# Sums moved to node order by a 0/1 matrix on TensorE, in an eight-layer graph network

## The chip, the cores and the metric

One core of one Trainium2 chip runs one program. The metric is the device time of a whole execution in microseconds. The kernel before took 10204.36 us, the median of 3 runs (10197.07 to 10204.97).

## What is computed

A graph of N = 6250 nodes with 128 features and 100000 edges, sorted by their destination dst. Eight layers of message passing stand one behind the other, in four blocks; each block normalises (layer norm and relu) and ends in a residual. Every layer gathers the source row of each edge and reduces per destination.

```python
h = relu(layernorm(x));  x = x + relu(h @ Wself.T + mean(h[src] by dst) @ Wneigh.T + b)        # k=0
h = relu(layernorm(x));  m = h[src] * edge_feat * bf(edge_weight) * cut
x = x + ssp(segment_prod(m, dst) @ W3 + b3)                                                  # k=1
h = relu(layernorm(x));  three times: h = mean(h[src] by dst) @ Wl + h @ Wr + b  (relu twice) # k=2,3,4
x = x + h
h = relu(layernorm(x));  three times:                                                        # k=5,6,7
    t = h @ W;  alpha = leaky(al_s[src] + al_d[dst] + al_e), with a self loop per node
    coef = softmax of alpha over the edges of each dst;  h = bn(leaky(sum(t[src] * coef) + b))
x = x + h
```

## The kernel before, in words

**Tiles.** The edges are 784 tiles of 128 (ET, padded), taken in 98 groups of eight (NG, HT). The nodes are 49 tiles of 128 rows (NT), and node work goes in seven chunks of seven tiles (NCH, CH; a chunk is CW = 896 columns). X, T, G and H are node-sized buffers of 49 x 128 columns, acc is as large and is addressed by rank (below). The edge layers are k = 0, 2, 3, 4 (mean, `SAGE`), k = 1 (product) and k = 5, 6, 7 (attention, `GAT`).

**A pass of a layer.** POOL issues one indirect DMA per tile (L620, in attention L641), which gathers 128 rows from the layer's table in DRAM into one of two halves of `rows`; a half is a group. DVE makes a 0/1 matrix `onehot` of a group's positions (L1240; in attention L1287, times the weight), PE multiplies rows by it into a half of PSUM (L903, in attention L923), and DVE adds the eight 128-column windows into acc at offsets that it loads into registers (L1256, L1307). POOL gathers into a half again when its products are through. The offset is a rank: the number of distinct destinations before, so that sorted edges fill the columns of acc without holes. In the product pass (k = 1) messages are built and scanned instead of summed, and stored as rows.

**Nodes and ranks.** Nodes without edges have no rank, so acc must be spread to node order. In pass 0 ACT stages three numbers per edge (L792, meta_buf: dst and position where it is a segment's last, and 1), PE multiplies them by the same onehot (L905), and DVE adds them in the same way into macc, a part of H. At the pass's end PE transposes them (L1072), DVE works out `cmap` (the rank of each node), first and last position and count, and POOL scatters and SP reloads a table of them (L657).

**Between two passes** (a turn, in the prediction's word). ACT copies acc chunk by chunk (L732), PE multiplies it by the layer's weights (L888), DVE copies the product out (L1380), SP stores it to seg_rows, and POOL gathers 49 tiles of rows by cmap (L677) into G. DVE then works through G by chunks (mean_layer; attention_layer, with batch statistics over all nodes and sums on PE) and writes H, the next layer's input, which SP stores as the next table. After layer 0, normalize and its root on ACT are in the chunk too; after layer 1 they work on the whole of X at once. In attention the last messages' maxima come first: 49 gathers of at_last (L664) stand behind the pass on POOL.

**A layer's own product** (h @ W). ACT copies a chunk of H (L708), PE transposes it (L862), ACT copies that (L699), PE multiplies (L868, L871), DVE copies it to T (L1218, L1231). In k = 0 and 2 this stands before the pass, in k = 3 to 7 inside the turn, chunk by chunk behind mean_layer and attention_layer; in attention T is also the table that is gathered.

**Staging in attention.** The messages' weights need all of alpha first, so the first SG = 30 groups are gathered, sent from `rows` to DRAM by DMAs that ACT issues (L811), and taken back during the weighted pass. POOL's third group waits for the first of them.

The order of the work is written out by hand, engine by engine, with semaphores; the lines of the profile are those of the block below. The two places that set the attention layers' start on ACT and POOL are:

```python
                    elif g < SG + 2:
                        pool.wait_ge(*staged_by(l, g - 2))
...
                elif k in by_chunks:
                    stage_chunks(k)
```

Of the kernel before, what the change touches and what calls it, by code (L numbers as in the profile page):

```python
# [21 lines left out]
ALU = mybir.AluOpType  # L22
# [36 lines left out]
SG = 30  # L59
FG = NG - SG  # L60
GROUP_WORDS = HT * D
SCATTER_AFTER = 8
SAGE = (0, 2, 3, 4)
# [3 lines left out]
def build(nc, a, out):  # L67
    ds = bass.ds
    with ExitStack() as ctx:
# [14 lines left out]
        seg_rows = dram("seg_rows", (NPAD, D))  # L84
        flats = dram("flats", (4, EPAD))
# [4 lines left out]
        node_table = dram("node_table", (NPAD, 4))  # L90
# [14 lines left out]
        meta_buf = sb("meta_buf", [P, BT * 3])  # L105
# [22 lines left out]
        node_info = sb("node_info", [P, NT * 4])  # L128
        cmap = sb("cmap", [P, NT], I32)
# [11 lines left out]
        ids_int = sb("ids_int", [P, NT], I32)  # L141
# [10 lines left out]
        H3 = H[:, 0:NT * D].rearrange("p (t f) -> p t f", f=D)  # L152
        stage = onehot[:].rearrange("p a b -> p (a b)")
        stage_in, stage_mid = stage[:, 0:CW], stage[:, 1024:1024 + CW]
        stage_out = rows[:].rearrange("p a b -> p (a b)")[:, 0:CW]
        macc = H[0:3, :]
        meta_t = G[:, 0:3 * ET]
# [25 lines left out]
        for l in range(3):  # L183
# [9 lines left out]
                      4: mat(M["agg2"]), 5: ident[:], 6: ident[:], 7: ident[:]}  # L193
# [41 lines left out]
        blocks = acc[0:TB, 0:4 * NB * P].rearrange("p (q b c) -> p q b c", q=4, c=P)  # L235
        pos_i = acc[:, 5600:5600 + ET].bitcast(I32)
        dst_t, last_t, srcf_t = scan_tmp(T, 0), scan_tmp(T, 1), scan_tmp(T, 2)
# [23 lines left out]
        info3 = node_info[:].rearrange("p (t c) -> p t c", c=4)  # L261
# [25 lines left out]
        info_turned = sem("info_turned")  # L287
        info_ready = sem("info_ready")
        info_scattered = sem("info_scattered")
        info_loaded = sem("info_loaded")  # L290
        info_cols = sem("info_cols")
# [3 lines left out]
        p_staged = sem("p_staged")  # L295
# [8 lines left out]
        meta_staged = sems("meta_staged", 2)  # L304
        meta_added = sems("meta_added", 2)
        c_staged = sem("c_staged")
        c_product = sem("c_product")
        c_copied = sem("c_copied")
        c_stored = sem("c_stored")
# [65 lines left out]


        by_chunks = {1: 0, 3: NCH, 4: 2 * NCH, 5: 3 * NCH, 6: 4 * NCH, 7: 5 * NCH}
        whole_inputs = {0: 1, 2: 2}

        table_parts = np.cumsum([1, NCH, 1] + 5 * [NCH]).tolist()  # L380

# [41 lines left out]
        def _(sp):  # L423
# [89 lines left out]
            for k in range(K):  # L513
                if k in GAT:
# [20 lines left out]
                    for g in range(2):  # L535
                        take_back(g)
# [1109 lines left out]
```

## Time and profile before

| | us |
|---|---|
| median of the 3 runs | 10204.36 |
| profiled execution | 10205.64 |
| its span | 10203.9 |
| PE busy | 5200.1 (51%) |
| PE weight loads | 3698.1 (36%) |
| DVE busy | 5257.5 (52%) |
| ACT busy | 1159.9 (11%) |
| POOL busy | 6947.8 (68%) |

The DMA queues moved 718.52 MB, 70 GB/s over the span. The mean granted clock of TensorE was 0.609 of full speed. Busy shares are averages over stages with different limits, so the table alone doesn't tell what a stage waits for; the stages are read apart below.

### The profile page before, as it was taken

Reading aid. Unit: us, or ns where it says so; the run is one execution under the profiler, and the core shown is the slowest. Engines: PE = TensorE matmul, PEld = TensorE weight load, DVE = VectorE, ACT = ScalarE, POOL = GpSimd, SP = SyncE. Lnnn points to the kernel's source line nnn. Section 1 sums busy time; section 2 is a strip of 40 time slices with the busy share of each in tenths; the row PEclk is TensorE's granted clock in tenths of the full one; section 3 lists DMA queues with packets and bytes.
Section 4 is the critical chain, followed back from the end, with each engine's and each line's share of the span. In section 5 each row is a group of like instructions: output and inputs, shape, how many; then the busy total and the mean of one; then the engine's idle time right before and its main releaser. Section 6 shows DMA issues by size and latency. Waiting matters only on the chain.

```text
span 10203.9 us, 101270 instructions
## 1 busy us (share of the span) xinstructions
PE 5200.1 (51%) x26044; PEld 3698.1 (36%) x26044; DVE 5257.5 (52%) x15574; ACT 1159.9 (11%) x1202; POOL 6947.8 (68%) x7020
## 2 busy tenths in 40 slices
PE   0888856777733334333343333844347453464533
PEld 0444422333323333333333333434343343433533
DVE  3444437777743333333343334976438774378744
ACT  0000006777720000000000000000010000100000
POOL 0677666777737776777777775777747777477775
PEclk9555557777765555555565555566555665556655
DMA  2111124444411112211121112232212321123311
GB/s 60 52 47 47 47 48 113 124 124 125 125 45 52 52 52 67 56 52 52 50 73 52 52 52 75 82 110 75 51 50 81 111 83 52 43 79 113 90 53 51
DMA packets 592271, 718.52 MB, mean 70 GB/s; under 512 B 141595, under 2 KB 456626, under 8 KB 591564
## 3 DMA queue, kind: packets, MB, share of 16 engines
q0 software_dynamic: 224224, 437.57, 16.4%
q1 hardware_dynamic: 354888, 231.66, 7.9%
q10 hardware_dynamic: 12960, 47.19, 1.2%
q8 instruction: 57, 0.93, 0.0%
q14 instruction: 142, 1.16, 0.0%
HBM read 556.42 MB, written 159.52 MB: 70 GB/s over the span
## 4 chain that ended last, share of the span: by engine, by line
POOL 53%; issue 20%; PE 15%; DVE 7%; DMA 3%; SPq 1%; ACT 1%; POOLq 0%; DVEq 0%; ACTq 0%
POOL rows L620 25%; POOL rows L641 21%; PE PS L932 5%; PE PS L903 3%; POOL G L677 3%; DVE T L1347 2%; PE PS L905 2%; PE PS L964 2%; DMA rows<-table,src_t 2%; POOL nd L664 1%; POOL at_first L626 1%; SPq L428 1%; PE PS L957 1%; PE PS L868 1%; DMA staged<-rows 1%
## 5 line engine op out<-in xcount | busy, mean ns | idle before, releaser
L620 POOL DMA_INDIRECT rows<-table,src_t x3920 | 3928.0, 1002 | 1803.8 <-issue 1211.2
L641 POOL DMA_INDIRECT rows<-table,src_t x2352 | 2251.2, 957 | 1036.8 <-issue 746.9
L903 PE MATMUL PS<-onehot,rows 128*128 128x128 f32 x6272 | 1718.9, 445 | 2011.4 <-DMA rows<-table,src_t 1966.8
L903 PEld LDWEIGHTS PS<-onehot,rows 128*128 128x128 f32 x6272 | 1410.8, 324 | 2428.4 <-issue 1479.4
L1256 DVE TENSOR_TENSOR acc<-acc,PS 128x128 f32 x3136 | 905.5, 289 | 2600.2 <-PE PS L903 1670.6
L923 PE MATMUL PS<-onehot,rows 128*128 128x128 f32 x3264 | 724.9, 412 | 1066.0 <-DMA rows<-table,src_t 996.9
L1307 DVE TENSOR_TENSOR acc<-acc,PS 128x128 f32 x2352 | 663.3, 282 | 805.9 <-PE PS L923 747.7
L923 PEld LDWEIGHTS PS<-onehot,rows 128*128 128x128 f32 x3264 | 670.4, 313 | 1116.2 <-DMA rows<-table,src_t 1058.8
L1287 DVE TENSOR_SCALAR onehot<-PS,loc_t,ex_t 128x128 f32<-128x128 f32 x2352 | 955.6, 408 | 0.6
L732 ACT ACTIVATE onehot<-acc 128x896 f32 x49 | 46.5, 949 | 5279.2 <-DVE acc L1256 3019.8
L932 PE MATMUL PS<-H,mats 128*128 128x512 f32 x784 | 514.4, 793 | 8.9 <-DVE H L1326 6.6
L677 POOL DMA_INDIRECT G<-seg_rows,cmap x343 | 377.8, 1101 | 171.2 <-issue 104.0
L1480 DVE TENSOR_SCALAR onehot<-PS,iota_col 128x1024 bf16<-128x1024 f32 x294 | 382.6, 1302 | 174.8 <-PE PS L996 174.8
L1492 DVE SCALAR_TENSOR_TENSOR H<-iota_row,srchi_t,PS 128x49 f32<-128x49 f32 x2352 | 465.1, 284 | 4.9 <-issue 4.9
L1006 PEld LDWEIGHTS PS<-als_bf,onehot 128*128 128x128 bf16 x7056 | 308.1, 119 | 425.7 <-DVE onehot L1480 269.3
L905 PE MATMUL PS<-onehot,meta_buf 128*3 128x128 f32 x1568 | 461.5, 398 | 0.0
L1006 PE MATMUL PS<-als_bf,onehot 128*128 128x49 bf16 x7056 | 347.1, 218 | 162.8 <-DVE onehot L1480 153.7
L1338 DVE TENSOR_TENSOR T<-T,PS 128x1024 f32<-128x1024 f32 x196 | 239.4, 1222 | 341.5 <-PE PS L957 341.5
L996 PE MATMUL PS<-cut_row,ones_bf 1*128 1x512 bf16 x588 | 302.0, 616 | 192.8 <-issue 192.7
L1240 DVE TENSOR_TENSOR onehot<-PS,loc_t 128x1024 f32<-128x1024 f32 x294 | 357.8, 1218 | 0.1
L964 PE MATMUL PS<-ident,T 128*128 128x128 f32 x784 | 192.9, 428 | 155.3 <-DVE T L1347 155.3
L923 PE MATMUL PS<-onehot,H 128*128 128x128 f32 x1440 | 238.8, 335 | 52.8 <-DVE onehot L1287 52.7
(297 smaller groups left out, 5968.6 us busy)
## 6 DMA issues: line engine op xcount, KB each, us to landing
rows<-table,src_t POOLq DMA_INDIRECT x6272
prod_rows<-onehot SPq DMA_DIRECT2D x98, 512.0 KB, 3.3
G<-in_edge_attr SPq DMA_DIRECT2D x97, 512.0 KB
staged<-rows ACTq DMA_DIRECT2D x90, 512.0 KB
H<-staged SPq DMA_DIRECT2D x90, 512.0 KB
seg_rows<-rows SPq DMA_DIRECT2D x49, 448.0 KB, 3.0
table<-H SPq DMA_DIRECT2D x21, 448.0 KB, 3.1
table<-T SPq DMA_DIRECT2D x21, 448.0 KB, 3.0
```

The lines of the kernel that those rows point to most:

```text
L620: pool.indirect_dma_start(rows[:, j, :], None, table[k % 2], at(src_t[:, t:t + 1]))\
L641: pool.indirect_dma_start(rows[:, g % 2 * HT + j, :], None, table[k % 2], at(src_t[:, t:t + 1]))\
L677: pool.indirect_dma_start(G3[:, t, :], None, seg_rows, at(cmap[:, t:t + 1])).then_inc(node_rows[t // CH], 16)
L903: last = mm(PS[:, o:o + D], rows[:, r, :], onehot[:, r, :], start=True, stop=True)
L905: last = mm(PS[0:3, 2048 + o:2048 + o + D], meta_buf[:, 3 * r:3 * r + 3], onehot[:, r, :], start=True, stop=True)
L923: last = mm(PS[:, o:o + D], block[:, j * D:(j + 1) * D], onehot[:, h * HT + j, :], start=True, stop=True)
L932: last = mm(bank(q), mat(M["W2" if n else "W1"]), rbf[:, q * 512:(q + 1) * 512], start=True, stop=True)
L1006: last = mm(PS[:, o:o + NT], hot_bf[:, h, j, :], als_bf[:, part * NT:(part + 1) * NT], start=(part == 0), stop=(part == 2))
L1256: tt(at, at, windows[:, j * D:(j + 1) * D], ALU.add).then_inc(done[h], 1)
L1287: return ts(onehot[:, c % 2 * HT + j, :], iota_ps, loc_t[:, t:t + 1], ex_t[:, t:t + 1], ALU.is_equal, ALU.mult)
L1307: tt(at, at, PS[:, h * 1024 + j * D:h * 1024 + (j + 1) * D], ALU.add).then_inc(added[h], 1)
L1492: last = stt(mask[:, j, :], iota_row[:, 0:NT], srchi_t[:, ds(e, 1)], cand[:, j, :], ALU.is_equal, ALU.mult, accum_out=als_t[:, ds(e, 1)])
```

## The change

- **Ranks to nodes on TensorE.** The 49 blocks of a 0/1 matrix say which rank of a 128-column window belongs to which node. They are made in pass 0 (make_perms on DVE, turn_perms on PE, copy_perms on ACT, into G), stored as perm_rows (3.2 MB) and loaded again in k = 2 and in each attention layer. A window starts at a tile's first rank, rank0. In the turn ACT copies the windows (L735), PE multiplies by the weights (weigh_ranks), ACT copies (L750), PE multiplies by the matrix (move_ranks), and DVE reads the result from PSUM. seg_rows, the row gathers by cmap and segments_out go.
- **Counts by a histogram.** A destination is split in two digits, which DVE turns into bf16 one-hots (node_digits L1362, L1364); PE multiplies the two and accumulates over all edges (L955). Rounds 15 to 63 of pass 0 take two groups each. At round 64 the counts are read, from 66 facts worked out, and rounds 68 to 80 make the matrix. meta_buf, its products and adds, and node_table go.
- **Own products inside the passes** of k = 0, 2, 3, 4: four tiles a round in rounds 0 to 13; DVE adds the bias as it takes them. The loops of these passes are written out. In k = 1 product, softplus and normalize go by chunks.
- **Attention.** The table is H, not h @ W; W comes in weigh_ranks. On ACT the seven copies of the own product (copy_turned) now stand ahead of the staging. SG goes from 30 to 34. The 49 gathers of at_last are issued before group 92, and self_weights stands three groups before the pass's end.

```diff
-SG = 30
+SG = 34
+GATHER_LAST_AT = NG - 6
+COUNT_FROM = 15
+FACTS_AT = COUNT_FROM + NG // 2
+PERM_FROM = FACTS_AT + 4
+PERM_BLOCKS = 4
...
+def product_tiles(k, c):
+    if k in SAGE:
+        return range(c * 4, min(NT, c * 4 + 4)), 2048, 2560
+    return range(c * CH, (c + 1) * CH), 0, 1024
...
-                      4: mat(M["agg2"]), 5: ident[:], 6: ident[:], 7: ident[:]}
+                      4: mat(M["agg2"]), 5: row_matrix[5], 6: row_matrix[6], 7: row_matrix[7]}
```

POOL and ACT:

```diff
+                    if g == GATHER_LAST_AT:
+                        gather_lasts(l)
...
-                if k in GAT:
-                    pool.wait_ge(last_st, 16 * (l + 1))
-                    pool.wait_ge(last_fill, l + 1)
-                    for t in range(NT):
-                        pool.indirect_dma_start(nd[:, 2 * t:2 * t + 2], None, at_last, at(lastpos[:, t:t + 1]),
...
-                for t in range(NT):
-                    if t == 0 or (t + 1) % CH == 0:
-                        pool.wait_ge(c_stored, 16 * min(NCH, (t + 1) // CH + 1) + turn[k] * (NCH * 16))
-                    pool.indirect_dma_start(G3[:, t, :], None, seg_rows, at(cmap[:, t:t + 1]))
...
+            def copy_windows(k, c):
+                done = turn[k] * NCH
+                s.load(rank0, rank0_row[0:1, c * CH:(c + 1) * CH])
+                first = [s.snap(r, min_val=0, max_val=ACCW - D) for r in rank0]
+                wait(s, ranks_ready, done + c - 1)
+                for j in range(CH):
+                    last = nc.scalar.activation(rows[:, c % 2 * HT + j, :], acc[:, ds(first[j], D)], ACT.Copy)
+                last.then_inc(windows_copied, 1)
...
+                copy_windows(k, 0)
+                for c in range(NCH):
+                    if c + 1 < NCH:
+                        copy_windows(k, c + 1)
+                    s.wait_ge(ranks_ready, done + c + 1)
+                    wait(s, nodes_ready, done + c - 1)
+                    nc.scalar.activation(by_rank_stage(c), by_rank(c), ACT.Copy).then_inc(ranks_copied, 1)
+                    if normalized and c > 0:
+                        chunk_sqrt(c - 1)
...
+            def softplus_products():
+                for c in range(NCH):
+                    copy_turned(1, c)
+                    s.wait_ge(ln_in, c + 1)
+                    step(nc.scalar.activation(G[:, c * CW:(c + 1) * CW], G[:, c * CW:(c + 1) * CW], ACT.Exp))
+                    nc.scalar.activation(G[:, c * CW:(c + 1) * CW], G[:, c * CW:(c + 1) * CW], ACT.Ln, bias=1.0)
+                    if c > 0:
+                        chunk_sqrt(c - 1)
...
+                if k != 1:
+                    for c in range(product_parts(k)):
+                        copy_turned(k, c)
```

PE and DVE:

```diff
+                    if 1 <= c <= product_parts(k):
+                        multiply_rows(k, c - 1)
+                    if c < product_parts(k):
+                        turn_rows(k, c)
+                    if k == 0:
+                        if COUNT_FROM <= c < FACTS_AT:
+                            for q in range(2):
+                                count_nodes(2 * (c - COUNT_FROM) + q)
...
+                for c in range(NG):
+                    add_group(k, c, c * HT)
+                    if c + 2 < NG:
+                        make_onehot(c + 2)
+                    if 1 <= c <= product_parts(k):
+                        take_product(k, c - 1)
+                    if k == 0:
+                        if COUNT_FROM <= c < FACTS_AT:
+                            for q in range(2):
+                                node_digits(2 * (c - COUNT_FROM) + q)
...
-                    g = chunk(G3, c)
-                    v.wait_ge(node_rows[c], (k + 1) * CH * 16)
-                    step(tt(g, g, chunk(T3, c), ALU.add))
+                    g = chunk(H3, c)
+                    v.wait_ge(nodes_ready, turn[k] * NCH + c + 1)
+                    step(tt(g, by_node(c).rearrange("p (t f) -> p t f", f=D), chunk(T3, c), ALU.add), nodes_used)
```

How the order of the instructions moves, first PE in the pass of layer 0, two groups of it. Before:

```order
L903 MATMUL PS<-onehot,rows 128x128 [waits meta_added0,meta_staged0,added0]
L905 MATMUL PS<-onehot,meta_buf 3x128
...
L903 MATMUL PS<-onehot,rows 128x128 [waits meta_staged1,added1,meta_added1,onehot_ready1,gathered1]
L905 MATMUL PS<-onehot,meta_buf 3x128
L903 MATMUL PS<-onehot,rows 128x128
```

and now, in a round that counts:

```order
L980 MATMUL PS<-onehot,rows 128x128 [waits added1,onehot_ready1,gathered1]
L980 MATMUL PS<-onehot,rows 128x128 x7
L955 MATMUL PS<-H 128x49 [waits count_ready0]
L955 MATMUL PS<-H 128x49 x7
L955 MATMUL PS<-H 128x49 [waits count_ready1]
L955 MATMUL PS<-H 128x49 x7
L980 MATMUL PS<-onehot,rows 128x128 [waits added0,onehot_ready0,gathered0]
```

The eight pairs of a group became eight products, and between two groups stand sixteen count products, which wait for digits. On DVE the digits stand behind the adds and the onehot of a round:

```order
L1334 TENSOR_TENSOR acc<-acc,PS 128x128
L1316 TENSOR_TENSOR onehot<-PS,loc_t 128x1024
L1362 TENSOR_TENSOR H<-PS,G 128x1024 [waits counted0]
L1364 TENSOR_TENSOR H<-PS,G 128x392 [waits dve]
L1362 TENSOR_TENSOR H<-PS,G 128x1024 [waits counted1]
L1364 TENSOR_TENSOR H<-PS,G 128x392 [waits dve]
L1325 TENSOR_LOAD seg_row
```

So the first two `L955` waits of a round are for what DVE makes after that round's last `L1334`.

Second, ACT at the start of layer 5, with the last chunks of the turn before it. Before:

```order
L692 ACTIVATE small<-small,cols 128x7 [waits var_ready]
L708 ACTIVATE onehot<-H 128x896 [waits p_turned,h_chunks]
L699 ACTIVATE onehot<-PS 128x896 [waits p_turned,p_product]
L811 DMA staged<-rows 128x1024 [waits gathered0]
L811 DMA staged<-rows 128x1024 [waits gathered1]
```

and now:

```order
L750 ACTIVATE onehot<-PS 128x896 [waits nodes_ready,ranks_ready]
L714 ACTIVATE small<-small,cols 128x7 [waits var_ready] x2
L722 ACTIVATE mid<-PS 128x896 [waits p_product,p_turned] x7
L840 DMA staged<-rows 128x1024 [waits gathered0]
L840 DMA staged<-rows 128x1024 [waits gathered1]
```

L714 is the root of normalize. The copies of the own product, which went chunk by chunk between the roots, stand together behind the last root and ahead of the first staging DMA.

## Rows read from the trace of the kernel before

**Rows 1.** The page, part 4: the chain that ended last, by engine
```profile
POOL 53%; issue 20%; PE 15%; DVE 7%; DMA 3%; SPq 1%; ACT 1%; POOLq 0%; DVEq 0%; ACTq 0%
```

**Rows 2.** Stretches: from:to, us, PE, PEld, DVE, ACT, POOL busy, PEclk, DMA, GB/s
```profile
265.60:1381.20 1115.60, 978.76 (x3196) 469.28 (x3195) 455.85 (x1641) 28.32 (x106) 768.85 (x784) 0.51 0.18 46
1381.20:1568.70 187.50, 36.11 (x187) 27.90 (x187) 90.55 (x128) 10.03 (x15) 100.40 (x99) 0.54 0.23 54
...
2851.60:3009.40 157.80, 43.61 (x196) 37.91 (x196) 67.72 (x21) 30.79 (x24) 48.84 (x50) 0.55 0.15 41
3009.40:4009.00 999.60, 372.94 (x1650) 346.15 (x1650) 346.27 (x880) 7.15 (x9) 739.64 (x784) 0.59 0.20 51
4009.00:4103.00 94.00, 51.10 (x247) 45.16 (x247) 43.66 (x49) 19.00 (x21) 51.04 (x49) 0.61 0.37 104
4103.00:5092.20 989.20, 364.90 (x1566) 338.63 (x1566) 342.01 (x876) 0.71 (x1) 739.62 (x784) 0.58 0.20 52
...
6174.90:6313.80 138.90, 78.55 (x359) 73.06 (x359) 90.97 (x103) 21.82 (x28) 52.45 (x50) 0.56 0.25 71
6313.80:7390.50 1076.70, 533.54 (x4129) 416.56 (x4129) 724.01 (x3299) 2.14 (x2) 799.16 (x833) 0.59 0.28 82
7390.50:7624.20 233.70, 113.09 (x555) 106.03 (x555) 83.73 (x87) 28.18 (x31) 105.87 (x99) 0.59 0.16 42
...
10011.00:10203.90 192.90, 60.38 (x310) 56.09 (x310) 81.72 (x83) 15.23 (x17) 106.06 (x98) 0.60 0.20 51
```

**Rows 3.** Timeline, a round of layer 3's pass: start, us, engine, line, [idle before <-releaser]
```profile
5073.89 3.78 PE L903 MATMUL PS<-onehot,rows 128*128 128x128 f32 x16 [5.94 <-DMA rows<-table,src_t]
...
5077.92 3.24 DVE L1256 TENSOR_TENSOR acc<-acc,PS 128x128 f32 x8 [5.38 <-PE PS L903]
...
5081.07 1.22 DVE L1240 TENSOR_TENSOR onehot<-PS,loc_t 128x1024 f32<-128x1024 f32 x1
```

**Rows 4.** Groups by line: count | busy us, mean ns | idle before, releasers
```profile
L1307 DVE TENSOR_TENSOR acc<-acc,PS 128x128 f32 x2352 | 663.3, 282 | 805.9 <-PE PS L923 747.7 <-issue 52.3 <-DVE acc L1307 0.5
L1006 PE MATMUL PS<-als_bf,onehot 128*128 128x49 bf16 x7056 | 347.1, 218 | 162.8 <-DVE onehot L1480 153.7 <-DVE H L1492 8.9
L732 ACT ACTIVATE onehot<-acc 128x896 f32 x49 | 46.5, 949 | 5279.2 <-DVE acc L1256 3019.8 <-DVE acc L1307 2106.8 <-PE PS L888 152.6
L792 ACT ACTIVATE meta_buf<-G 128x24 f32 x98 | 21.7, 222 | 1069.4 <-PE PS L905 1069.4
L692 ACT ACT_TABLE_LOAD x5 | 6.4, 1283 | 0.1
```

**Rows 5.** Timeline of DVE, the turn after layer 4 and layer 5's start
```profile
6181.94 3.23 DVE L1256 TENSOR_TENSOR acc<-acc,PS 128x128 f32 x8 [8.15 <-PE PS L903]
...
6229.02 1.09 DVE L1409 TENSOR_TENSOR G<-G,rcount 128x896 f32<-128x896 f32 x1
...
6240.98 1.08 DVE L1409 TENSOR_TENSOR G<-G,rcount 128x896 f32<-128x896 f32 x1
...
6374.85 2.48 DVE L1480 TENSOR_SCALAR onehot<-PS,iota_col 128x1024 bf16<-128x1024 f32 x2 [58.35 <-PE PS L996]
```

**Rows 6.** Timeline of DVE, the turn after layer 5
```profile
7532.43 0.29 DVE L1559 TENSOR_SCALAR H<-H,rowmask 128x128 f32<-128x128 f32 x1
...
7554.61 1.09 DVE L1577 TENSOR_TENSOR H<-H,acc 128x896 f32<-128x896 f32 x1
...
7602.29 1.09 DVE L1218 COPY T<-PS 128x896 f32<-128x896 f32 x1 [5.60 <-PE PS L871]
...
7611.11 1.09 DVE L1218 COPY T<-PS 128x896 f32<-128x896 f32 x1 [5.61 <-PE PS L871]
```

**Rows 7.** The chain of waits at the start of layer 5
```profile
6328.58 8.88 DMA staged<-rows
```

**Rows 8.** Timeline of POOL in layer 5: gathers behind a wait
```profile
6337.72 0.94 POOL L641 DMA_INDIRECT rows<-table,src_t  x1 [4.27 <-DMA staged<-rows]
...
6722.05 0.94 POOL L641 DMA_INDIRECT rows<-table,src_t  x1 [5.45 <-PE PS L923]
```

More of the change, by code:

```diff
@@ L127, in build @@
         rowmask = sb("rowmask", [P, 1])
[L128 to L129 removed]
+        mid = sb("mid", [P, CW])
+        plocal = sb("plocal", [P, NT])
+        count = sb("count", [P, NT])
+        rank0_row = sb("rank0_row", [1, NT], I32)
         firstpos = sb("firstpos", [P, NT], I32)
@@ L726, in stage_segments, with copy_turned, chunk_sqrt @@
-            def stage_segments(k):
+            def copy_turned(k, c):
+                tiles, at, _ = product_tiles(k, c)
+                w = len(tiles) * D
+                s.wait_ge(p_turned, c + 1 + products_before[k])
+                wait(s, p_product, c + products_before[k])
+                nc.scalar.activation(mid[:, 0:w], PS[:, at:at + w], ACT.Copy).then_inc(p_copied, 1)
+            def chunk_sqrt(c):
+                sqrt(1.0 / D, stat1[:, c * CH:(c + 1) * CH], stat1[:, c * CH:(c + 1) * CH])
@@ L892, in edge_pass @@
[L892 to L907 removed]
+                turn_rows(k, 0)
@@ new lines, in count_nodes, with sum_facts @@
+            def count_nodes(q):
+                h = q % 2
+                pe.wait_ge(count_ready[h], q // 2 + 1)
+                for j in range(HT):
+                    last = mm(counts_ps, lo_digit[:, h, j, :], hi_digit[:, h, j, :], start=(q == 0 and j == 0),
+                              stop=(q == NG - 1 and j == HT - 1))
+                last.then_inc(counted[h], 1)
+            def sum_facts():
+                pe.wait_ge(facts_in, 1)
+                for q, (m, x) in enumerate(((before, plocal), (ones, plocal), (before, count), (ones, count))):
+                    last = mm(facts_ps[:, q, :], m[:], x[:], start=True, stop=True)
+                last.then_inc(facts_out, 1)
@@ new lines, in _, with add_group @@
+            seg_regs = [v.alloc_register(f"segment{j}") for j in range(HT)]
+            def add_group(k, c, t, between=None):
+                h, i = c % 2, c // 2
+                before_pass = turn[k] * ITERS * HT
+                v.load(seg_regs, seg0_row[0:1, t:t + HT])
+                first = [v.snap(r, min_val=0, max_val=ACCW - D) for r in seg_regs]
+                v.wait_ge(*multiplied_by(k, c))
+                for j in range(HT):
+                    if j == 0:
+                        wait(v, added[1 - h], (i + h) * HT + before_pass)
+                    else:
+                        v.wait_ge(added[h], i * HT + j + before_pass)
+                    at = acc[:, ds(first[j], D)]
+                    tt(at, at, PS[:, h * 1024 + j * D:h * 1024 + (j + 1) * D], ALU.add).then_inc(added[h], 1)
+                    if between:
+                        between(j)
@@ L1284, in weighted_pass, with make_perms @@
+            def make_perms(m):
+                wait(v, perm_turned, m)
+                for j in range(min(PERM_BLOCKS, NT - m * PERM_BLOCKS)):
+                    b = m * PERM_BLOCKS + j
+                    last = ts(perm_in[:, j * D:(j + 1) * D], iota_ps, plocal[:, b:b + 1], None, ALU.is_equal)
+                last.then_inc(perm_made, 1)
             def weighted_pass(k):
```

550 lines of the change are left out of this document (258 added, 292 removed).

## The prediction

> **What bounds the kernel now.** I read the chain that ended last first. POOL holds 53% of it, another 20% is "issue", its pause between two gathers, and PE has 15% [rows 1]. Then I cut the span by the indirect DMAs on POOL: a pass is the 784 gathers of one layer, a turn is the stretch from a pass's last gather to the next pass's first. In the passes of layers 2 to 4 POOL is the limit: layer 3 takes 989.2 us for 784 gathers, 10.1 us per group of eight, with PE busy for 365 us of it. The pass of layer 0 takes 1115.6 us with PE busy for 978.8. In the turns the gather machinery stands still: 187.5 us after layer 0, 157.8 after layer 1, 94.0 after layer 2 and much the same after layer 3, 138.9 after layer 4, 233.7 after layer 5 and the same after layer 6, 192.9 at the end [rows 2]. So two things can pay: a pass of layer 0 at POOL's pace, and shorter turns.
>
> **Pass of layer 0.** The 784 thin products with meta_buf go, and so do their DVE adds. A plain round is: products of a group 4.0 us until DVE's first add, eight adds 3.2, the one-hot 1.2, together 8.4 us [rows 3]. The digits are behind that on DVE, and here is the catch: PE runs a round's two count groups before the next group's products, the counts wait for digits, DVE makes these after the adds of the same group, and the adds wait for that group's products. In 49 rounds PE and DVE take turns. Two digit pairs cost 2 x (1.22 + 0.47 + 0.06) = 3.5 us (0.47 is 1.22 scaled to 392 columns), the last eight count products 0.5 (their kind runs at 347.1/7056 = 0.05 us each when dense, 0.22 alone, which bounds this by 0.4 and 1.8 [rows 4]). The round is 8.4 + 3.5 + 0.5 = 12.4; the granted clock of such a pass is 0.58 [rows 2], so now and then the products run at 2.4 instead of 1.2 GHz and I take 12.1. That is 49 x 2.0 = 98 us over POOL's pace. The 13 rounds with permutation blocks take turns in the same way, with four 128-column tests (1.3) and four transposes (1.2): 11.0, or 12 us in all. Own products in rounds 1 to 13 add some 3 us of PE and 0.7 of DVE to rounds with room; they cost nothing, since their waits were satisfied a round before. 989 + 98 + 12 = 1099: 16 us gained. The prologue loses a few 784-column operations and one load: between 0 and 3 us, taken as 0.
>
> **The turns.** New chain: last gather to last add 10.3 us (layer 4: 6174.9 to 6185.2) [rows 2, 5], then ACT copies seven windows for each of two chunks, PE, ACT, PE, and DVE starts. ACT's copy of 128 columns is not in the trace; 24 columns take 0.222 and 896 take 0.949 us [rows 4], which gives 0.31 between them. With the register load a chunk of windows is 3.1 us and ACT's whole chunk 4.2. PE needs 3.4 us at 1.2 GHz for seven products, twice a chunk: 6.8, or 3.7 at 2.4. The turns now show a granted clock of 0.54 to 0.61, a mixture of both levels [rows 2]. So a chunk is 4.2 to 6.8 us, I take 5.5, the middle, and 13 us until DVE's first operation.
> By the Trainium skill, "ScalarE: Activation LUTs", section "What ACT_TABLE_LOAD costs", an ACTIVATE without a pointer bias is 186 ns + 0.833 ns per column and neighbours overlap by 93 ns. It gives 206 ns for 24 columns where the row has 222. Seven windows would take 1.4 us instead of 2.2, and the sum would be up to 25 us lower.
>
> - After layers 2 and 3: 10.3 + 13 + 6 x 5.5 + 2.9 (three DVE operations) + 3.1 (store and start, my estimate) = 62.3. Gain 2 x 31.7 = 63.
> - After layer 4, DVE's chain per chunk decides: now 11.9 us from chunk to chunk, less the bias add and the copy to T, 1.1 each: 9.7 [rows 5]. 10.3 + 13 + 7 x 9.7 + 3.1 = 94.3. Gain 45.
> - After layer 0 the same chain, the node-table round trip and the row gathers gone: 94.3. Gain 93.
> - After layer 1 the 49 gathers stay; the whole-tile operations become chunks. A chunk on DVE is 1.1 + 0.65 + 6.9 to the variance, 1.8 for root and scale; and then it waits, since ACT's next copy_turned stands behind this root and PE needs 3.4 after it: 13.7 us. From the first gather: 36 to the first variance, 5 x 13.7, 10.6 for the last chunk without a product, 4 to the next gather = 119. Gain 39. ACT now changes tables three times a chunk (1.28 us each [rows 4]), 2.6 of it inside DVE's 6.9: hidden.
> - Layer 2's pass no longer starts behind its own row products: 999.6 becomes 989.2. Gain 10.
>
> **Attention layers, where something is lost.** The 49 gathers of at_last move inside the pass: 49 x 1.29 (1076.7/833) = +63. Worse, ACT now has seven copy_turned ahead of its first staging DMA, and POOL's third group waits for that DMA. DVE frees the product buffer only in attention. Counted from the last normalised chunk, the memset of attr_att and the first take end at 3.1, and then a round of product, transposes and copy takes 8.8, the pace these products show now [rows 6]. Two copies are through by then, five follow: the seventh ends at 3.1 + 5 x 8.8 = 47, that is 44 after the first gather. Staging takes 8.9 [rows 7], so POOL goes on at 53.2 where it went on at 23.9 (6337.7 against 6313.8) [rows 2, 8]: +29.3 us; in layer 5 +35, because there even the first copy stands behind the last root. With SG at 34 POOL's wait of 5.4 us before its 33rd group goes [rows 8]. The start of the picks stays: it waits 58 us for a PE spread whose row comes behind the attribute load [rows 5], and this covers the late products. Passes: 3 x (63 + 29.3 - 5.4) + 5.4 = 266 lost.
> The turn after: 10 + 13 + 6 x 5.5 + 4.7 (four DVE operations and the row mask) = 60.7 to the mask, 22.2 from it to the scale (7532.4 to 7554.6 [rows 6]), 7 x 2.25 without products between, 3.3 = 102.0 against 233.7: 2 x 131.7 = 263. At the end 60.7 + 22.2 + 28.3 (21 operations of 1.1, and the store) = 111.2 against 192.9: 82.
>
> **Sum.** 16 + 93 + 39 + 10 + 63 + 45 - 266 + 263 + 82 = 345 us. The profiled execution took 10205.6 us, so 9860.6; the median shown is 1.3 lower: 9859.
>
> **Rivals.**
> A. The counting does not bind, because PE gets 2.4 GHz or DVE's digits run faster. For: PE has 16 cheap products more. Against: 8.4 us of the round are measured and 1.7 are left for 4 us of work. Time 9859 - 98 = 9761. Chance 0.08.
> B. Staging is not held, or only briefly: at 2.4 GHz the products halve. Against: the copies to T stand 8.8 us apart now, with PE nearly always busy between them [rows 6]. 9859 - 93 = 9766, at 2.4 GHz about half of that, 9812. Chance 0.14.
> C. ACT's small copies bind the turns: register steps between them make a chunk 7.5 us. For: nothing in the trace is like them. Five turns x 6 x 2.0 = 60: 9919. Chance 0.2.
> D. **Slower than before.** The mean layers' rounds on PE, DVE lose their loops and become straight code for 392 groups. If feeding that code cost more than the 1.7 us per round that POOL leaves between 8.4 and 10.1, all four passes stretch. It decides from 345/392 = 0.9 us beyond that, 2.6 us a round. Against: attention's rounds are straight code already and wait 52.3 us for "issue" in 294 groups, 0.18 each [rows 4]. At 3 us a round: 9859 + 392 x 1.3 = 10369. Chance 0.03. The Trainium skill, "Runtime: NRT & Kernel Launch", section "Instruction fetch mechanics", says straight code is prefetched in order and mostly hidden, while a taken branch can break the prefetch. The trace agrees as far as those 0.18 us.
> E. The row order by matrix replaces the gathers, but the turn keeps another wait (the 3.2 MB permutation load, one more 12 us stall per attention layer): 9859 + 36 = 9895. Chance 0.05.
>
> **Numbers.** Forecast, with sizes as above, 0.5; the rivals 0.5. Range: downward the counting rounds (98) or the staging (93), with PE at 2.4 GHz in the turns (5 x 6 x 1.0 = 30); upward C's 60 or PE at 1.2 GHz in every turn (5 x 6 x 1.3 = 39): 9740 to 9950. What a measurement can tell from no change is 0.2%, some 20 us. Only D reaches it, and D would have to fall between: faster 0.96, same 0.01, slower 0.03.
>
> **What would show it.** In the new profile: rounds with L955 12.1 us apart and the first and last ones 10.1; an idle time of POOL near 30 us before the third group of layers 5 to 7, ended by a staging DMA; the turns at 94, 119, 62, 62, 94, 102, 102; ACT's L735 near 0.31 us. It is wrong if the counting rounds run at 10.1, if POOL's wait in attention is as short as now, or if the turns after layers 2 and 3 are over 75 us.

## The result, and the profile after

The changed kernel takes 9771.08 us, the median of 4 runs (9764.6 to 9773.36), beside 10204.67 us of the kernel before: a ratio of 0.9575, with an interval of 0.9563 to 0.9587. The profiled execution has a span of 9771.3 us against 10203.9, so 432.6 us are to be accounted for. The forecast was 9859 us with a range of 9740 to 9950: the direction held, the time lies inside the range, and the gain is 88 us larger than forecast.

The page of the changed kernel, part 4, the chain that ended last:

```profile
POOL 52%; issue 21%; PE 13%; DVE 11%; SPq 1%; DMA 1%; ACT 0%; DVEq 0%; POOLq 0%; ACTq 0%
```

POOL and issue are still 73% of the chain together, as before [rows 1]. Cut in the same way as [rows 2], with the same columns:

```profile
259.80:1337.40 1077.60, 427.84 (x2540) 395.65 (x2540) 524.55 (x1149) 14.88 (x26) 739.83 (x784) 0.59 0.19 51
1337.40:1429.70 92.30, 38.09 (x213) 36.58 (x214) 67.87 (x79) 19.66 (x64) 0.00 (x0) 0.65 0.14 37
...
2711.90:2827.90 116.00, 33.10 (x147) 29.61 (x147) 69.83 (x79) 41.78 (x44) 52.59 (x49) 0.54 0.22 59
2827.90:3817.00 989.10, 384.50 (x1699) 358.37 (x1699) 346.68 (x888) 7.44 (x13) 739.69 (x784) 0.60 0.21 55
3817.00:3861.70 44.70, 27.95 (x212) 27.33 (x212) 23.76 (x30) 16.49 (x56) 0.05 (x1) 0.81 0.27 75
...
5885.80:5977.00 91.20, 42.34 (x236) 40.80 (x237) 67.99 (x79) 19.17 (x64) 0.00 (x0) 0.71 0.14 37
...
7148.90:7236.90 88.00, 60.01 (x450) 57.97 (x450) 60.82 (x65) 26.57 (x67) 0.00 (x0) 0.83 0.14 38
7236.90:8408.70 1171.80, 569.39 (x4332) 452.20 (x4332) 738.95 (x3314) 6.97 (x8) 853.09 (x882) 0.59 0.28 81
...
9672.40:9771.30 98.90, 51.19 (x408) 50.03 (x408) 65.85 (x70) 24.84 (x65) 0.00 (x0) 0.78 0.12 34
```

Subtracted from the stretches of before, and set beside the terms of the prediction (turns by the layer they follow):

| term | forecast gain, us | measured, us |
|---|---|---|
| start, up to the first gather | 0 | 5.8 |
| pass of layer 0 | 16 | 38 |
| turn 0 | 93 | 95 |
| turn 1 | 39 | 42 |
| pass of layer 2 | 10 | 10.5 |
| passes of layers 1, 3 and 4 | 0 | -0.4 |
| turns 2 and 3 | 63 | 98 |
| turn 4 | 45 | 48 |
| three attention passes | -266 | -287 |
| turns 5 and 6 | 263 | 289 |
| end | 82 | 94 |
| sum | 345 | 433 |

Three things are seen in the rows. The pass of layer 0 is 88 us above layer 2's, so it is still not at POOL's pace. The shortest turn has a granted clock of 0.81 where the turns of before had 0.54 to 0.68 (the 0.68 is the turn after layer 3, which took 93.6 us and is not among the rows). And in attention both gains and losses are large. A round of the counting stretch, in the timeline of the changed kernel (columns as in [rows 3]; POOL and weight loads left out):

```profile
601.36 0.52 PE L955 MATMUL PS<-H 128*128 128x49 bf16 x8 [6.28 <-DVE H L1364]
...
603.09 0.51 PE L955 MATMUL PS<-H 128*128 128x49 bf16 x8 [1.21 <-DVE H L1364]
...
603.42 3.76 PE L980 MATMUL PS<-onehot,rows 128*128 128x128 f32 x16
...
607.32 3.24 DVE L1334 TENSOR_TENSOR acc<-acc,PS 128x128 f32 x8 [4.29 <-PE PS L980]
...
613.48 0.52 PE L955 MATMUL PS<-H 128*128 128x49 bf16 x8 [6.29 <-DVE H L1364]
```

From one first L955 to the next are 12.12 us. PE stands idle for 6.3 us until DVE has made digits (L1364), and DVE then for 4.3 us until PE has made the next products: they take turns.

The turn after layer 2, one chunk of it on each engine:

```profile
3840.22 1.09 DVE L1496 TENSOR_TENSOR H<-PS,rcount 128x896 f32<-128x896 f32 x1 [0.54 <-PE PS L940]
...
3841.51 1.73 PE L940 MATMUL PS<-onehot,G 128*128 128x128 f32 x14
...
3843.07 1.73 PE L932 MATMUL PS<-mats,rows 128*128 128x128 f32 x14
3843.35 1.09 DVE L1496 TENSOR_TENSOR H<-PS,rcount 128x896 f32<-128x896 f32 x1 [0.25 <-PE PS L940]
3843.74 1.51 ACT L735 ACTIVATE rows<-acc 128x128 f32 x7 [1.11 <-issue]
...
3844.64 1.73 PE L940 MATMUL PS<-onehot,G 128*128 128x128 f32 x14
```

A chunk takes 3.13 us. PE has no gap between L940 and L932: seven products take 1.6 us, twice (the rows have 14 records for seven fp32 products). ACT's seven windows take 1.51 together.

### The profile page after: what moved, and what is told of

Same layout as the page of the kernel before. It is cut to its first block, busy times and chain, and to the rows that moved or that the text cites. A ratio compares the mean times of both kernels' runs of the same rounds, so it can differ in the third digit from the quotient of the medians.

```text
span 9771.3 us, 95144 instructions
## 1 busy us (share of the span) xinstructions
PE 4612.8 (47%) x25947; PEld 3624.8 (37%) x25947; DVE 5238.5 (54%) x15043; ACT 1189.0 (12%) x1461; POOL 6513.7 (67%) x6626
## 4 chain that ended last, share of the span: by engine, by line
POOL 52%; issue 21%; PE 13%; DVE 11%; SPq 1%; DMA 1%; ACT 0%; DVEq 0%; POOLq 0%; ACTq 0%
POOL rows L651 26%; POOL rows L681 22%; PE PS L1018 5%; DVE T L1457 2%; PE PS L1050 2%; PE PS L980 2%; POOL nd L664 1%; POOL at_first L657 1%; SPq L459 1%; DVE acc L1334 1%; PE PS L1043 1%; DVE H L1362 1%; PE PS L906 1%; DVE onehot L1316 1%; DVE H L1364 1%
## 5 line engine op out<-in xcount | busy, mean ns | idle before, releaser
L1334 DVE TENSOR_TENSOR acc<-acc,PS 128x128 f32 x5488 | 1559.6, 284 | 3383.5 <-PE PS L980 2141.2
L980 PE MATMUL PS<-onehot,rows 128*128 128x128 f32 x6272 | 1451.5, 425 | 2119.2 <-DMA rows<-table,src_t 2119.2
L980 PEld LDWEIGHTS PS<-onehot,rows 128*128 128x128 f32 x6272 | 1350.3, 327 | 2208.6 <-DMA rows<-table,src_t 2208.6
L1009 PE MATMUL PS<-onehot,rows 128*128 128x128 f32 x3072 | 688.5, 415 | 1197.5 <-DMA rows<-table,src_t 1142.8
L1009 PEld LDWEIGHTS PS<-onehot,rows 128*128 128x128 f32 x3072 | 637.0, 316 | 1242.2 <-DMA rows<-table,src_t 1192.2
L1316 DVE TENSOR_TENSOR onehot<-PS,loc_t 128x1024 f32<-128x1024 f32 x392 | 477.0, 1218 | 6.4 <-DMA table<-H 5.8
L735 ACT ACTIVATE rows<-acc 128x128 f32 x343 | 73.9, 295 | 2880.9 <-issue 2877.1
L1082 PE MATMUL PS<-cut_row,ones_bf 1*128 1x512 bf16 x588 | 302.1, 616 | 13.3 <-DVE nd L1563 13.3
L1009 PE MATMUL PS<-onehot,H 128*128 128x128 f32 x1632 | 261.7, 328 | 30.3 <-DVE onehot L1403 29.9
L1009 PEld LDWEIGHTS PS<-onehot,H 128*128 128x128 f32 x1632 | 255.2, 246 | 37.6 <-issue 37.5
L1018 PEld LDWEIGHTS PS<-H,mats 128*128 128x128 f32 x784 | 182.2, 257 | 202.5 <-issue 182.0
## 6 DMA issues: line engine op xcount, KB each, us to landing
G<-perm_rows SPq DMA_DIRECT2D x4, 3136.0 KB, 12.1
```

Source lines behind the costliest of these rows:

```text
L980: last = mm(PS[:, o:o + D], rows[:, r, :], onehot[:, r, :], start=True, stop=True)
L1009: last = mm(PS[:, o:o + D], block[:, j * D:(j + 1) * D], onehot[:, h * HT + j, :], start=True, stop=True)
L1018: last = mm(bank(q), mat(M["W2" if n else "W1"]), rbf[:, q * 512:(q + 1) * 512], start=True, stop=True)
L1316: tt(onehot[:, h * HT:(h + 1) * HT, :], iota_ps.unsqueeze(1).broadcast_to([P, HT, D]), loc_t[:, t:t + HT].unsqueeze(2).broadcast_to([P, HT ...
L1334: tt(at, at, PS[:, h * 1024 + j * D:h * 1024 + (j + 1) * D], ALU.add).then_inc(added[h], 1)
```

## The experiments

Two chips had a part in this. The first four experiments ran on one where the kernel before takes 10203.38 us, as it did for the result above, so they are compared with the changed kernel's 9771.08. The others met a chip on which the kernel before takes 12150 us and the changed one 11579 (after_again); they are compared with the runs on that chip alone.

**lag_counts.** PE counts a round's digits behind the next group's products.

```diff
-                        if COUNT_FROM <= c < FACTS_AT:
+                        if COUNT_FROM < c <= FACTS_AT:
                             for q in range(2):
-                                count_nodes(2 * (c - COUNT_FROM) + q)
+                                count_nodes(2 * (c - 1 - COUNT_FROM) + q)
```

> Edit: PE multiplies a round's digits one round later, behind the next group's products; nothing else moves. Theory (PE and DVE take turns: PE waits for digits that DVE can only make after its adds, which wait for PE): the rounds that count go from 12.0 us to POOL's 10.0, the pass of layer 0 from 1077.6 to about 989 to 992, the whole from 9771 to about 9685. Rival (the work itself, 8.1 us of DVE a round and PE's sixteen count products, is too much for a round): rounds stay above 11.5 us and the whole above 9750.

Measured: 9684.92 us (ratio 0.9491, 0.9475 to 0.9507), 86 us below the changed kernel. Its stretch of layer 0, and a round:

```profile
259.30:1250.20 990.90, 423.34 (x2540) 401.50 (x2540) 525.20 (x1149) 14.89 (x26) 741.48 (x784) 0.62 0.21 56
```

```profile
604.45 3.79 PE L980 MATMUL PS<-onehot,rows 128*128 128x128 f32 x16 [5.48 <-DMA rows<-table,src_t]
...
608.03 0.87 PE L955 MATMUL PS<-H 128*128 128x49 bf16 x16
608.37 3.24 DVE L1334 TENSOR_TENSOR acc<-acc,PS 128x128 f32 x8 [2.11 <-PE PS L980]
...
614.44 3.39 PE L980 MATMUL PS<-onehot,rows 128*128 128x128 f32 x16 [5.54 <-DMA rows<-table,src_t]
```

Both engines do the same work as before the edit, DVE 525 us of it in the pass, and now PE waits for the gathers only. The order made the 86 us, not the work; the rival falls.

**early_staging.** ACT issues a staging DMA between the copies of the own product.

```diff
+                if k in GAT:
+                    for c in range(NCH):
+                        copy_turned(k, c)
+                        if 0 < c < NCH - 1:
+                            stage(c - 1)
...
-                    for g in range(SG):
+                    for g in range(NCH - 2, SG):
```

> Edit: in attention ACT issues a staging DMA after each of the copies 2 to 6 of the own product, instead of all staging after the seventh copy. Theory (POOL's third group waits for a DMA that stands behind seven copies 8.8 us apart): POOL's wait of 31.9 us before the third group falls to about 4.5, as in the kernel before; each attention pass 27 us shorter, the whole 9771 to about 9690. Rival (the copies are now late instead, and picks or the attribute load start later): the 27 us come back before the weighted part, the whole stays within 10 us of 9771.

Measured: 9699.79 us (ratio 0.9506, 0.949 to 0.9521), 71 us less. POOL's waits for staging in layer 6, first of the changed kernel, then of this one:

```profile
7288.53 0.94 POOL L681 DMA_INDIRECT rows<-table,src_t  x1 [31.95 <-DMA staged<-rows]
```

```profile
7247.85 0.95 POOL L681 DMA_INDIRECT rows<-table,src_t  x1 [4.20 <-DMA staged<-rows]
7271.11 0.95 POOL L681 DMA_INDIRECT rows<-table,src_t  x1 [3.55 <-DMA staged<-rows]
```

The theory holds, with 24 us a layer and not 27: with the long wait gone, POOL meets a second one of 3.6 us before its 33rd gather. Nothing came back elsewhere: 71 us is three times 24.

**late_self.** The multiplication of T by the self weights stands behind the last add.

```diff
-                step(tt(T3, T3, exs_n.unsqueeze(2).broadcast_to([P, NT, D]), ALU.mult))
...
                     weighted_pass(k)
+                    step(tt(T3, T3, exs_n.unsqueeze(2).broadcast_to([P, NT, D]), ALU.mult))
                     attention_layer(k)
```

> Edit: the one operation of self_weights that multiplies T by the self weights (128x6272, 6.7 us on DVE) goes behind the pass's last add; the small ones stay. Theory (one indirect DMA of POOL took 7.04 us instead of 0.94 while this operation ran, because DVE held what POOL needs): no such gather is left, each attention pass is 6.1 us shorter, and the operation hides in DVE's 9.6 us of idle time before the first chunk; the whole 9771 to about 9753. Rival (the long gather was chance or a full queue): passes unchanged, and the turn the same or up to 6.7 us longer each, the whole 9771 to 9791.

Measured: 9755.58 us (ratio 0.9561, 0.9546 to 0.9577), 15.5 us less. The changed kernel, DVE and POOL near the end of layer 6's pass:

```profile
8392.95 0.94 POOL L681 DMA_INDIRECT rows<-table,src_t  x1 [0.30 <-issue]
...
8393.73 6.69 DVE L1637 TENSOR_TENSOR T<-T,small 128x6272 f32<-128x6272 f32 x1
8394.20 7.04 POOL L681 DMA_INDIRECT rows<-table,src_t  x1 [0.30 <-issue]
8401.49 3.22 DVE L1334 TENSOR_TENSOR acc<-acc,PS 128x128 f32 x8 [1.07 <-issue]
```

And late_self, the same operation in the turn after layer 5:

```profile
7155.77 6.68 DVE L1693 TENSOR_TENSOR T<-T,small 128x6272 f32<-128x6272 f32 x1
7165.20 1.09 DVE L1644 TENSOR_TENSOR H<-PS,T 128x896 f32<-128x896 f32 x1 [2.74 <-PE PS L940]
```

A gather that began 0.47 us after the DVE operation ended 0.82 us after it. Moved, the operation lies in time in which DVE waits for PE anyway, and no gather near the end is long: layer 6's last 48 take 59.7 us instead of 65.8.

**more_windows.** Five more copies of acc for each chunk of seven.

```diff
+                spare = [rows[:, c % 2 * HT + CH, :], onehot[:, c % 2 * HT + CH, :]]
+                spare += [mid[:, (c % 2 * 3 + j) * D:(c % 2 * 3 + j + 1) * D] for j in range(3)]
+                for j, to in enumerate(spare):
+                    nc.scalar.activation(to, acc[:, ds(first[j], D)], ACT.Copy)
```

> Edit: five more 128-column copies of acc per chunk in copy_windows, to places nobody reads. Theory (a chunk of the turns after layers 2 and 3 is set by ACT and PE together at 3.1 to 3.2 us; seven copies take 1.50 us, 0.2 each): a chunk there becomes about 4.2 us, these two turns go from 44.7 to about 52, the others, where DVE's own operations set the pace, gain 1 to 2 us each; the whole 9771 to about 9793. Rival (PE alone sets the pace and ACT has room): 1 us a turn, 9778. Second rival (such a copy costs 0.3 us as its record says): 54 in those turns, 9800.

Measured: 9780.01 us (ratio 0.9584, 0.9568 to 0.96), 9 us more, nearest the first rival's 7. The interval alone doesn't exclude the theory's 22; the chunks do. In the turn after layer 2 they are 3.19 us apart, not 4.2:

```profile
3844.07 1.79 PE L936 MATMUL PS<-mats,rows 128*128 128x128 f32 x14
3844.34 1.09 DVE L1500 TENSOR_TENSOR H<-PS,rcount 128x896 f32<-128x896 f32 x1 [0.32 <-PE PS L944]
...
3844.88 0.30 ACT L737 ACTIVATE onehot<-acc 128x128 f32 x1
...
3847.53 1.09 DVE L1500 TENSOR_TENSOR H<-PS,rcount 128x896 f32<-128x896 f32 x1 [0.32 <-PE PS L944]
```

ACT had about 1 us of room in a chunk; PE alone sets 3.13. The theory, that ACT binds as well, was wrong. This turn grew by 2.5 us in all, most of it ahead of the third chunk, where the first windows stand in the way of PE.

**port**, and **port_again** with the same kernel. One idle operation per round in two passes.

```diff
+                    if k == 3 and 18 <= c < NG - 2:
+                        step(tt(mid[:], mid[:], mid[:], ALU.max))
+                    if k == 2 and 18 <= c < NG - 2:
+                        step(tt(mid[:], PS[:, 2048:2048 + CW], mid[:], ALU.max))
```

> Edit: one idle DVE operation (128x896, 1.09 us, its result is not used) in each of 78 rounds of two passes; in layer 2's pass it reads PSUM and one SBUF tensor, in layer 3's two SBUF operands; layer 4's pass has none. DVE is busy for some 4.5 us of a 10 us round, so by DVE's time alone neither costs anything. Theory (an operation with two operands in SBUF keeps POOL from issuing its indirect DMA): layer 3's pass grows from 989.8 by 0.5 to 1.1 us per operation, 40 to 85 us, with gathers of up to 2 us in it; layer 2's stays at 989. Rival (any long DVE operation does it, or none): both grow alike, or neither.

> The same kernel as port. There 57 gathers of layer 3's pass took over 1.0 us (up to 1.85) and none of layer 2's or 4's, but POOL had time left in each round, so no pass grew. Where POOL sets the pace: theory, the excess of those gathers (13 us there) goes into the time, layer 3's pass 10 to 40 us longer than layer 4's, layer 2's the same as layer 4's. Rival: the passes of layers 2 and 3 alike.

Measured: 11577.31 and 11589.58 us, one run each, beside 11578.89. The passes of layers 2, 3 and 4 in port:

```profile
2933.10:4051.60 1118.50, 387.44 (x1699) 359.29 (x1699) 423.83 (x966) 7.45 (x13) 741.17 (x784) 0.60 0.17 49
4097.50:5215.60 1118.10, 388.76 (x1699) 360.00 (x1699) 421.27 (x958) 7.45 (x13) 754.29 (x784) 0.58 0.17 46
5262.00:6381.30 1119.30, 391.61 (x1699) 362.92 (x1699) 343.18 (x888) 7.44 (x13) 741.22 (x784) 0.56 0.17 46
```

```profile
4600.91 0.95 POOL L651 DMA_INDIRECT rows<-table,src_t  x1 [0.30 <-issue]
...
4601.62 1.08 DVE L1348 TENSOR_TENSOR mid<-mid 128x896 f32<-128x896 f32 x1
4602.16 1.35 POOL L651 DMA_INDIRECT rows<-table,src_t  x1 [0.30 <-issue]
```

POOL's busy time is 13 us larger in layer 3's pass alone: 57 of its gathers took over 1.0 us, up to 1.85, and none of layer 2's or 4's; in port_again it was 55. The times, from one run each, tell nothing here; the traces do. The lines of layer 3's pass show one: the gather begun during the operation takes 1.35 us and again ends 0.81 us behind it, while the one begun before it keeps its 0.95. So it is two operands in SBUF that do it, not DVE's being busy. The price is far below what was expected, 13 us and not 40 to 85, since an operation as short as 1.08 us costs only the gather that begins during it, and that one only what is left of it. And the passes are alike: a group took 11.4 us on this chip, not 10.1, and POOL had room. That the excess becomes time where POOL sets the pace is therefore shown by late_self alone.

The kernel before shows the same without any edit. In its product pass a gather takes 0.94 us beside a DVE operation of 1.22 us that reads PSUM, and 1.94 beside one that reads two operands in SBUF (`G<-G,rows`):

```profile
1601.70 1.22 DVE L1338 TENSOR_TENSOR T<-T,PS 128x1024 f32<-128x1024 f32 x1 [3.19 <-PE PS L957]
1602.09 0.94 POOL L620 DMA_INDIRECT rows<-table,src_t  x1 [0.30 <-issue]
...
1608.60 1.22 DVE L1319 TENSOR_TENSOR G<-G,rows 128x1024 f32<-128x1024 f32 x1
1608.69 1.94 POOL L620 DMA_INDIRECT rows<-table,src_t  x1 [0.30 <-issue]
```

All 57 gathers that began during an L1319 took over 1.0 us. Of 107 that began during an L1338, more than 0.2 us before its end, none did.

**sg30.** SG = 30 instead of 34.

> Edit: 30 staged groups instead of 34. The prediction counted 5.4 us gained in each attention layer by 34. The trace of the changed kernel has a wait of 6.3 us for PE before the 37th group, where the kernel before had 5.4 before the 33rd. Theory (the wait only moved): each attention pass within 3 us of 1171.8 and the whole within 10 us of 9771. Rival (34 removes a wait of its own): 5.4 us more per layer, 9787.

Measured: 11582.95 us (ratio 0.9537, 0.9523 to 0.9552) beside 11578.89 of the changed kernel (0.9528, 0.9513 to 0.9542): no difference that the intervals show, and the rival's 16 us aren't excluded by them. But the trace shows the wait move with SG. With 30 staged groups it stands before the 33rd group of layer 6 (the row), with 34 before the 37th, there 340.17 us long. So long is this wait on this chip, whichever group it is before:

```profile
8949.28 0.95 POOL L681 DMA_INDIRECT rows<-table,src_t  x1 [343.45 <-PE PS L1009]
```

On the first chip, too, it stands in the changed kernel before the 37th group of layer 6, about as long as before the 33rd in the kernel before (5.45 us in layer 5 [rows 8]):

```profile
7709.29 0.94 POOL L681 DMA_INDIRECT rows<-table,src_t  x1 [6.30 <-PE PS L1009]
```

**products_first.** The thirteen parts of the own product ahead of the first group in layers 2, 3 and 4.

```diff
             def edge_pass(k):
+                if k > 0:
+                    turn_rows(k, 0)
+                    for c in range(product_parts(k)):
+                        multiply_rows(k, c)
+                        if c + 1 < product_parts(k):
+                            turn_rows(k, c + 1)
```

> Edit: in layers 2, 3 and 4 all thirteen parts of the own product stand ahead of the first group on PE and DVE instead of one a round. Theory (inside the pass they use room that a round has; ahead of it they hold PE, so POOL's third group waits, and POOL never catches up): 13 parts at some 3.5 us, less 12 us until the first rows are there, 25 to 35 us more per layer, the whole 9850 to 9875. Rival (PE starts on them while the turn still runs, so nothing is held): within 15 us of 9771.

Measured: 11652.67 us (ratio 0.9596, 0.958 to 0.9612), 74 us above the changed kernel there, 25 a layer. POOL's wait before layer 2's third group:

```profile
2984.20 0.95 POOL L651 DMA_INDIRECT rows<-table,src_t  x1 [23.50 <-PE PS L986]
```

In layers 3 and 4 the same wait is 32.9 and 25.6 us. So the rounds do have room for the thirteen parts, and ahead of the first group these cost POOL their time at once.

**combined, combined_again.** lag_counts, early_staging and late_self in one kernel.

> Edit: the three edits lag_counts, early_staging and late_self together. Theory (they act on different stretches and add): 9771 - 86 - 71 - 15.5 = 9598. Rival (with staging early, the T multiply or the copies meet another wait in attention): above 9615.

> The same kernel as combined. On the chip where the passes run at POOL's pace: theory (the three edits add) 9598 us; rival (they meet another wait in attention) above 9615. On the other chip the pass of layer 0 gained 21 us instead of 86, since its rounds stood at 11.4 us anyway.

Measured: 11475.49 us (ratio 0.9446, 0.9433 to 0.9459) and 11478.82 (0.9445, 0.9433 to 0.9458), beside the changed kernel:

> The changed kernel itself, so that the next three have it beside them on their own chip (the runs port, sg30, products_first and combined met a chip on which the kernel before takes 12151 us): ratio to the kernel before 0.957 where that one takes 10204 us, some 0.953 on the other chip, which is what port and sg30 showed there.

That one took 11578.89 us, so the three edits together give 100 us on this chip, and the version beats both kernels. It was not run on the first chip. That the parts add up to 173 us there, as each alone gave, stays open; here layer 0's pass had little to gain, since its plain rounds already stood at 11.4 us.

**combined_late_perm.** The load of the matrix behind the last staged group's return.

```diff
-                    for g in range(2, SG // 2):
-                        take_back(g)
+                    for g in range(2, SG):
+                        take_back(g)
                     sp.wait_ge(last_fill, l + 1)
                     sp.dma_start(G[:], perm_rows).then_inc(perm_loaded, 16)
-                    for g in range(SG // 2, SG):
-                        take_back(g)
```

> Edit on combined: in attention the 3.2 MB load of the matrix goes behind the last staged group's way back instead of in its middle. Theory (POOL's pause before its 450th DMA is 6.65 us instead of the usual 2.1 because the load was in the way): that pause falls to about 2.1 to 2.7, each attention pass 4 us shorter, 12 us in all. Rival (the pause has another cause, or the load now meets another gather): within 4 us of combined.

Measured: 11478.99 us (ratio 0.9446, 0.9432 to 0.9461), the same as combined_again. It decides nothing: on this chip the pause in question is 0.6 us in combined already. On the first chip the row of the changed kernel, 9 us after the load's issue in layer 6, is this:

```profile
7857.01 0.94 POOL L681 DMA_INDIRECT rows<-table,src_t  x1 [6.65 <-issue]
```

The five kernels on the first chip have this pause fifteen times, three attention layers each. In two of them it began 1.1 and 1.2 us after the load's issue and was 2.74 and 2.99 us long, near the 2.3 to 2.7 of the kernel before, which has no such load. In the other thirteen it began 1.6 to 3.0 us after the issue and was 4.7 to 7.8 us long; the load in layer 6 landed 11.8 us after its issue. So the load being in the way is likely, but no run without it at this pace was made.

## Why the prediction was right, and where its sizes were off

**Pass of layer 0: right mechanism, 22 us too dear.** The taking of turns was there, and lag_counts shows it. POOL's groups 20 to 67 are 561.0 us:

```profile
463.50:1024.50 561.00, 208.88 (x1496) 191.32 (x1496) 318.46 (x610) 0.00 (x0) 354.71 (x377) 0.58 0.17 44
```

That is 11.94 us each over 47 groups, where 49 of 12.1 were priced. The same 47 take 474.7 us in layer 2, so 86 us are stretching, and the whole pass is 88 us above layer 2's and not 98; POOL's lead of two groups absorbed the rest. The 12 us for the 13 permutation rounds are the part that failed: priced at 11.0, they stood 10.3 us apart on DVE on average, and POOL kept its pace through them.

**Turns: the chunk of 5.5 us was the step that failed.** It measured 3.13. Two of its parts were too dear. For ACT the whole was put at 4.2 us, with 0.31 for a copy of 128 columns. One has a record of 295 ns, but seven of them take 1.51 us, since they overlap, and more_windows shows some 1 us of room beyond. The sentence on the Trainium skill's page "ScalarE: Activation LUTs", section "What ACT_TABLE_LOAD costs", which gave 1.4 us for seven, was closer than my interpolation, but its "up to 25 us lower" isn't borne out: more_windows gave ACT some 1 us more in each chunk and the whole grew by 9 us, so 0.7 us less there could not have been worth 25.

What made the chunks short is PE. For it I took a mixture of both clock levels, from turns in which it worked in pieces, and even my 3.7 us at 2.4 GHz was 0.6 too much. The granted clock of the turns after layers 2 and 3 is 0.81, mostly the upper level, and a chunk is two times 1.6 us, below both ends of my 4.2 to 6.8. In the turn after layer 0 both levels stand in one trace: seven products took 3.35 us after PE had been idle for 8.47, and 1.73 in a stretch without gaps:

```profile
1357.77 1.73 PE L932 MATMUL PS<-mats,rows 128*128 128x128 f32 x14
...
1369.53 3.35 PE L932 MATMUL PS<-mats,rows 128*128 128x128 f32 x14 [8.47 <-ACT rows L735]
```

The sum of it: 6 x 2.4 us too much in two turns is 28 of the 35 us; the rest is DVE's first operation, 19.8 us after the last gather and not 23.3. In turns 5, 6 and the end DVE's four operations set the pace, 4.5 us a chunk and not 5.5, which is 6 us each, and the first operation came 3.6 us earlier; the statistics between mask and scale took 18.2 us and not 22.2, which is 4 more. Turn 6 gave 3 us less than turn 5 (91.2 against 88.0), at a granted clock of 0.76 against 0.83.

**Turns 0, 1 and 4: right to 3 us each**, since there DVE's own chain decides: 9.78 us from chunk to chunk against 9.7 in turn 0. In turn 1 DVE waits 2.8 to 3.0 us a chunk for PE, as forecast, and a chunk is 13.1 to 13.3 us against 13.7.

**Attention passes: 21 us too cheap.** The staging hold was right: in layer 6 POOL went on 51.6 us after the layer's first gather, where 53.2 was forecast, and early_staging shows the cause. It cost 24 us and not 29.3, since a shorter wait before the 33rd gather went with it. The 5.4 us more for layer 5 did not come: POOL's wait there was 31.78 us, as in the other two. Three things were missed. That the wait of 5.4 us goes with SG at 34 failed. It stands before the 33rd group, not the 33rd gather as the prediction has it, and it moved to the 37th group and is 6.3 us long. The T multiplication inside the pass costs a gather 6.1 us; the prediction had no term for it. And there is the pause of 6.65 us behind the matrix load, where the same gather of the kernel before has 2.69; the experiments make the load the likely cause and don't prove it. Against a forecast of 1163.6 us for layer 6, these are 6.0 (5.4 counted as gained, and 0.6 more), 6.1 and 4.0, against the 5.4 that staging cost less and one usual pause of 2.2 us fewer: together some 8 us, which is what the measured 1171.8 lie above the forecast.

**Rivals.** A fell by the counting rows, B by the wait of 31.95 us, C by the copies at 0.2 us apart. D fell too: the straight-line passes of layers 2 to 4 take 989.1 to 989.8 us, as the loop of layer 3 did [rows 2]. The trace so agrees with the Trainium skill, "Runtime: NRT & Kernel Launch", section "Instruction fetch mechanics", which has straight code prefetched. E came true by a third at most, 4 us a layer instead of 12.

**The range.** Its lower end was made of the counting (98 us) and the staging (93 us), and both cost nearly what was forecast. The gain that was missed lies in the turns after layers 2, 3, 5 and 6 and at the end, for which the range had 30 us. So the time fell inside the range, but in part for other reasons than those that set it.

## What to carry to other kernels

Where two engines hand work to each other in every round, look for a product that waits in a queue ahead of independent work; a lag of one round needed no new buffer and gave 86 us here. When work moves from a starved engine into a stretch where that engine runs without gaps, price it at both clock levels and not at the old mixture (here 5.5 us a chunk was priced and 3.13 measured). A busy PE alone doesn't promise the upper level: in the pass of layer 0 before, PE was busy for 978.8 of 1115.6 us at a granted clock of 0.51 [rows 2]. And an in-order queue that issues a DMA the bottleneck waits for should issue it before anything that waits for others: seven copies ahead of one DMA cost 24 us a layer.

## What the runs showed of the hardware

A DVE operation with two operands in SBUF holds up indirect DMAs that POOL begins during it: 7.04 us instead of 0.94 beside one of 6.69 us, and 57 long gathers beside 78 operations of 1.08 us, while none was long beside 78 that read PSUM. A gather held up in this way ended 0.8 us after the DVE operation. The gathers beside the product pass's operations of the kernel before say the same: 57 of 57 long beside those with two SBUF operands, 0 of 107 beside those that read PSUM. The Trainium skill, "SBUF — State Buffer", section "SBUF: two separate sides", says that a DVE operation with two SBUF inputs and a GpSimd operation that reads SBUF exclude each other for the whole instruction. The runs agree for a gather that begins second. In the other direction they don't: the DVE operation at 4601.62 in port began during a gather (4600.91 to 4601.86) and took its usual 1.08 us. Nor are two operands the only case. Eight gathers of the kernel before began during an L1418, a DVE operation of 0.63 us with one operand of 128x896 in SBUF, and took 1.35 to 1.36 us.

Two chips differed by 19% on the kernel before (10204 and 12150 us). On the slower one the instructions took as long and POOL issued at the same pace, but a group took 11.4 us, and in attention POOL stood for 340 us before the 37th group. Of the 1810 us that the changed kernel lost there, 1306 are in the three attention passes and 389 in those of layers 2 to 4. The waits before DVE's adds grew from 3024 to 3755 us in all; 3200 of these the trace puts down to "remote", that is, to no instruction of this core. The cause was not found. The two chips show that an edit's worth can hang on the chip: lag_counts made the pass of layer 0 87 us shorter on one, and on the other it got only 22 us shorter with all three edits (1148.1 to 1125.6).
